# Gated delta attention between two spline layers: the values' tanh, the last passes of the next unit and the turned keys take other places in a written order

## What is computed

```python
qkvz = (x @ W_qkvz)                     # q, k, v (2 heads), z (2 heads) per key head
q, k, v = silu(causal_conv4(q, k, v))   # 4 taps along the tokens
q, k = INV**2 * rms_norm(q), INV * rms_norm(k)
def step(S, inp):                       # over the 512 tokens
    S = S * exp(g_t)
    delta = (v_t - k_t @ S) * beta_t
    S = S + outer(k_t, delta)
    o = q_t @ S
out = (silu(z) * rms_norm(o) * norm_w) @ W_out
x = x + out
```

## Time and profile before

| what | value |
|---|---|
| median of 3 runs | 3598.28 us (3597.3 to 3602.36) |
| the profiled execution's own time | 3600.39 us |
| its span | 3598.6 us |
| PE (matmul) busy | 3364.6 us, 93% |
| DVE busy | 2293.9 us, 64% |
| ACT busy | 2106.6 us, 59% |
| POOL busy | 2267.9 us, 63% |
| granted TensorE clock, mean | 0.978 |

### The profile page before, as it was taken

One profiled execution on the slowest core, in us unless ns is written; L12 is line 12 of the kernel. 1 busy time (PEld: TensorE's weight loads), 2 busy tenths in 40 slices (PEclk: granted clock), 3 DMA queues, 4 the chain that ended last, 5 costly groups with the idle time before them and its releaser, 6 DMA issues. The chain is left out here.

```text
span 3598.6 us, 77659 instructions
## 1 busy us (share of the span) xinstructions
PE 3364.6 (93%) x29092; PEld 2467.3 (69%) x29092; DVE 2293.9 (64%) x4402; ACT 2106.6 (59%) x5699; POOL 2267.9 (63%) x2680
## 2 busy tenths in 40 slices
PE   5997799999999999999999999999999999995998
PEld 3886366767676777667676767676767676773787
DVE  4664666666666767666666666666666666663564
ACT  3443566666666666666666666666666666662343
POOL 2111677777777777777777777777777777772110
PEclk8998899999999999999999999999999999997999
DMA  3524121212121212222222222222222222112321
GB/s 135 184 48 70 46 69 57 97 56 92 58 89 60 89 60 88 68 86 67 80 67 79 71 76 75 72 79 68 79 68 79 69 80 67 60 60 81 137 48 36
DMA packets 217314, 274.48 MB, mean 76 GB/s; under 512 B 91248, under 2 KB 127344, under 8 KB 215792
## 3 DMA queue, kind: packets, MB, share of 16 engines
q1 hardware_dynamic: 207680, 253.60, 22.6%
q0 software_dynamic: 4464, 14.36, 1.1%
q10 hardware_dynamic: 4800, 1.56, 0.3%
HBM read 180.12 MB, written 89.16 MB: 75 GB/s over the span
## 5 line engine op out<-in xcount | busy, mean ns | idle before, releaser
L2097 ACT ACTIVATE at_t<-at_inv 128x512 f16<-128x512 f32 x768 | 462.5, 602 | 398.1 <-PE at_inv L1905 391.9
L2337 DVE TENSOR_TENSOR at_pml<-at_prod,at_cst 128x256 f16<-128x256 f32 x768 | 323.0, 421 | 146.2 <-PE at_prod L1682 137.3
L2483 POOL TENSOR_TENSOR at_gm<-at_cst,at_gates 128x512 fp32r<-128x512 f32 x256 | 261.5, 1042 | 233.5 <-PE at_misc L1682 233.5
L1682 PE MATMUL at_proj<-x_hi,at_w_hi 128*128 128x512 f16 x1024 | 390.6, 381 | 2.8 <-PEq L1268 2.8
L1682 PE MATMUL at_proj<-x_lo,at_w_hi 128*128 128x512 f16 x1024 | 391.5, 382 | 0.0
L1682 PE MATMUL at_proj<-x_hi,at_w_lo 128*128 128x512 f16 x1024 | 391.5, 382 | 0.0
L2259 DVE SCALAR_TENSOR_TENSOR rows<-at_misc,first_tab,rows 128x512 f32<-128x512 f32 x256 | 191.7, 749 | 245.9 <-PE at_misc L1682 245.9
L1903 PE MATMUL at_inv<-at_pml,at_t 128*128 128x64 f16 x3072 | 286.8, 194 | 31.9 <-DVE at_pml L2337 31.6
L1903 PEld LDWEIGHTS at_inv<-at_pml,at_t 128*128 128x128 f16 x3072 | 223.1, 98 | 136.0 <-DVE at_pml L2337 83.3
L2215 DVE SCALAR_TENSOR_TENSOR at_cv_v<-at_proj,at_cw,at_cv_v 128x511 f32<-128x511 f32 (+2 forms) x384 | 287.5, 749 | 21.8 <-ACT at_cv_v L2021 8.3
L1682 PE MATMUL at_prod<-at_t,at_nlhi 128*128 128x64 f16 (+1 forms) x3584 | 287.8, 197 | 6.4 <-ACT at_t L2097 3.2
(11 more groups left out here) (323 smaller groups left out, 10278.4 us busy)
## 6 DMA issues: line engine op xcount, KB each, us to landing
rows<-x SPq DMA_DIRECT2D x64, 1024.0 KB, 5.5
x<-rows SPq DMA_DIRECT2D x64, 1024.0 KB, 4.6
at_gb<-decays SPq DMA_DIRECT2D x64, 512.0 KB, 3.7
at_raw_w<-w_qkvz SPq DMA_DIRECT2D x48, 512.0 KB, 7.5
ffn_weights<-ffn_w SPq DMA_DIRECT2D x1, 11776.0 KB, 34.8
ffn_w<-ffn_weights POOLq DMA_DIRECT2D x4, 2688.0 KB, 23.5
at_raw_o<-w_out SPq DMA_DIRECT2D x16, 512.0 KB, 3.5
f_xnext<-x_in SPq DMA_DIRECT2D x4, 1024.0 KB, 5.2
```

Source lines behind the costliest of these rows:

```text
L1682: return nc.tensor.matmul(out, lhsT, rhs, start=start, stop=stop)
L2097: own["a_t"].up(A(grown(t16[:, s % R].rearrange("p a t -> p (a t)"), s // R), grown(psT[s % R], s // R), ACT.Copy))
L2337: own["d_p"].up(V.tensor_tensor(pml[:, level - 1, g].rearrange("p (c b a m) -> p c b a m", c=CH, a=2, m=m)[:, :, :, 0, :], psP[:, 0:S // 2 ...
L2483: last = G.tensor_tensor(gm[:, k], incl.unsqueeze(1).to_broadcast([P, CH, P]), new_gates[:, g, at:at + CH, h:h + 1].to_broadcast([P, CH, P ...
```

## The change

On PE, the six `fill` lists of steps 11 to 15 are dealt out anew: Z1's 24 passes end as before in step 13 but lie 4, 4, 2 in place of 5, 2, 3 in steps 11 to 13; `turn_k` goes from step 12 to step 11; V0's 12 passes go from 4 and 8 in steps 14 and 15 to 2, 3, 3, 4 in steps 12 to 15. On ACT, V1's tanh leaves step 5 and stands at the end of the slot before, between the last squares of `at_aqk` and `copy_t(j + 1, 1)`; K's tanh goes from step 6 to step 4, ahead of `gated(j - 1, 1)`; Z0's from step 9 to step 8; `square_k` from step 12 to 11. On DVE, `silu_z(Z0)` goes from step 12 to step 10. POOL's and SP's passes are not edited.

```diff
@@ -1848,18 +1848,20 @@
                     fill[8].append(gates_in(Z1_U, 0, 5))
                     fill[9].append(gates_in(Z1_U, 5, 10))
                     fill[10].append(gates_in(Z1_U, 10, 14))
-                    fill[11].append(gates_in(Z1_U, 14, 19))
-                    fill[12].append(gates_in(Z1_U, 19, 21))
-                    fill[13].append(gates_in(Z1_U, 21, 24))
+                    fill[11].append(gates_in(Z1_U, 14, 18))
+                    fill[12].append(gates_in(Z1_U, 18, 22))
+                    fill[13].append(gates_in(Z1_U, 22, 24))
                 if behind:
                     for h in range(R):
                         fill[3 + 2 * h].append(lambda h=h: turn_gated(h, j - 1))
                     for c in range(WPROD):
                         fill[7 + c].append(lambda c=c: out_product(c, j - 1))
                 if has_prep:
-                    fill[12].append(turn_k)
-                    fill[14].append(parts(V0_U, 0, 4))
-                    fill[15].append(parts(V0_U, 4, 12))
+                    fill[11].append(turn_k)
+                    fill[12].append(parts(V0_U, 0, 2))
+                    fill[13].append(parts(V0_U, 2, 5))
+                    fill[14].append(parts(V0_U, 5, 8))
+                    fill[15].append(parts(V0_U, 8, 12))
                     gap[0].append(parts(V1_U, 0, 3))
                     gap[1].append(lambda: gram_of(j + 1))
                     gap[2].append(lambda: decay(0))
@@ -2118,18 +2120,17 @@
                 if has_prep:
                     steps[2].append(lambda: tap(Q_U))
                 if behind:
-                    for h in range(R):
-                        steps[2 + 2 * h].append(lambda h=h: gated(j - 1, h))
-                if has_delta:
-                    steps[5].append(lambda: tanh(V1_U, j - 1))
+                    steps[2].append(lambda: gated(j - 1, 0))
                 if has_prep:
-                    steps[6].append(lambda: tanh(K_U))
+                    steps[4].append(lambda: tanh(K_U))
+                if behind:
+                    steps[4].append(lambda: gated(j - 1, 1))
                 if has_prep:
                     steps[9].append(lambda: tanh(Q_U))
                 if has_delta:
-                    steps[9].append(lambda: tanh_z(Z0_U))
+                    steps[8].append(lambda: tanh_z(Z0_U))
                 if has_prep:
-                    steps[12].append(square_k)
+                    steps[11].append(square_k)
                 if has_delta:
                     steps[14].append(lambda: tanh_z(Z1_U))
                 for s in range(R, STEPS + 1):
@@ -2186,6 +2187,8 @@
                     for h in reversed(range(R)):
                         own["a_sqo"].up(squares(CH - 1, h))
                 if has_prep:
+                    tanh(V1_U)
+                if has_prep:
                     copy_t(j + 1, 1)
                 if ends:
                     for h in range(R):
@@ -2325,7 +2328,7 @@
                     for c in range(WPROD):
                         steps[7 + c].append(lambda c=c: out_add(c, j - 1))
                 if has_delta:
-                    steps[12].append(lambda: silu_z(Z0_U))
+                    steps[10].append(lambda: silu_z(Z0_U))
                 for s in range(R, STEPS):
                     if has_delta:
                         g, level = s % R, s // R
```

## The result

The changed kernel takes **3582.69 us** (median of 4 runs, 3576.59 to 3586.05) against 3598.78 of the kernel before (median of 4 runs, 3597.3 to 3602.36): a ratio of 0.995, 95% interval 0.9936 to 0.9964. That is 16.1 us less; 3587 was forecast, 11 less than the 3598.28 that the three runs had on which the forecast was made. The profiled execution took 3586.05 in place of 3600.39, its span is 3584.2 in place of 3598.6: 14.3 and 14.4 less.

A forecast was written before the change was run, and what follows sets the result against it. Slots were taken as paced by PE's instruction stream plus small waits, split slots by POOL's list. 63 slots losing 0.57 (+36 us) and split slots giving 46.5 make -11 us: 3598.28 to 3587, range 3562 to 3604.

The forecast's parts named there:

- The sum: Whole kernel: 63 middle slots lose 0.57 each, +36 us, split slots give back 46.5 us, together -11 us.
- 46.5 us of the split slots gone: 15 split slots, 3.1 us each over an ordinary slot's 43.87, become like the others: -46.5 us.
- The price of an ordinary slot: In each middle slot `turn_kn` comes at 1529.49 against 1528.92, 0.57 us later; +36 us over 63 slots.
- POOL leaves the path: POOL gains 3.3 us of lead, so it no longer delays `scale_k` in ordinary or split slots.
- the rival in which POOL does not come out early: Split slots keep their wait while each slot pays 0.57, +36 us: 3634; chance 0.05.
- The clock: PE: waits of 0.8 bring no fall, seven split-slot falls go; rival: falls in ordinary slots, 3634, chance 0.06.
- were taken out of the one place where a chain of ACT had to be covered: Between residual(1) and `turn_kn`, V0's eight passes become four; PE has 0.87 us less work and waits about 0.8.
- the four transposes fit into the wait for the mask: PE's step 11: `turn_k`'s four transposes, swapped for one pass, fit into the wait for DVE's mask.
- the lower bound of the price: Slot price 0.25 us if ACT's 0.29 wait for POOL and a similar slack at residual(1) come off: 3567.
- My first rival: Passes fill the waits of steps 12 and 13, ordinary slots stay at 43.9, only 46.5 us go: 3552; chance 0.12.

The follow-up runs named there:

- experiment 1: Kernel before with only V1's tanh moved to the slot's end and K's to step 4, no pass or silu moved: 3524.08 us, ratio 0.9795.
- experiment 2: The full change with V1's tanh back in step 5, K's back in step 6 and the gates as before: 3630.72 us, ratio 1.0091.
- experiment 7: experiment 1 plus `turn_k` in step 11 and Z1's passes 4, 4, 2; squares, silu and V0 stay: 3537.0 us, ratio 0.9841.
- (4): experiment 3 with Z0's silu also back in step 12 on DVE: 3555.43 us, ratio 0.9883.
- experiment 3: The full change with V0's passes back to 4 and 8 in steps 14 and 15: 3579.74 us, ratio 0.995.
- experiment 5: Kernel before with V1's tanh alone moved to the slot's end, K's tanh left in step 6: 3536.27 us, ratio 0.9837.

## Why the prediction was right, and where it was not

**The sum, against what was found.** In the beat: 46.5 us of the split slots gone, forecast and found (56 of its 61 slots, split or not, take 44.34 to 44.41, and five ordinary ones 44.49 to 44.68). The price of an ordinary slot was forecast as 0.57, and is 44.385 less 43.865, **0.52**. Over 61 slots that makes 46.5 less 31.7, 14.8, against 14.0 between the first and last rows of the beat (the longer slots are some of the rest); the forecast had 46.5 less 36 for 63 slots, 10.6. So the beat gives some 3 us more than forecast. Outside the beat the sum had no more than the price of two slots, and there are three terms: the first slot is 3.9 shorter, the phase starts 1.6 later (433.78 against 432.19), and 1.9 is lost behind the beat's last start (16.3 earlier, 3197.4 to 3181.1, where the span is shorter by 14.4). 14.0 + 3.9 - 1.6 - 1.9 is the 14.4 of the spans. That the three nearly cancel each other is luck. The medians are 16.1 apart, 1.7 more than the profiled executions: two runs of the changed kernel took 3576.59 and 3579.54, two 3585.84 and 3586.05, the last of which is the profiled one. What the two shorter ones did otherwise, no trace shows.

**The first slot was missing in the sum.** I counted every slot as an ordinary or a split one, and it is neither: its wait of POOL for V1's tanh was 7.95, twice the usual, and it had a fall of the clock of its own, the eighth beside the seven of the split slots. Against its 3.9 stands what is lost at the end of the phase, where the changed kernel has a stretch at the lower clock (columns as above):

```profile
3228.00:3232.00 4.00, 3.76 (x40) 3.21 (x38) 1.67 (x4) 2.49 (x5) 3.84 (x5) 0.57 0.00 0
```

The kernel before has none in its last slots up to 3260 (its granted clock is 1.00 from 3224 to 3260), and behind that both have two such stretches of equal length, 6.8 and 47.8. One fall more, at the 1.5 of the split slots, would be most of the 1.9; no run shows that it is.

**POOL leaves the path, right.** Experiments 1 and 2 show it from both sides: with the tanhs moved the split slots are as short as the others, with or without the passes; with the passes moved alone they stay longer. For the rival in which POOL does not come out early, 3634, experiment 2 is the nearest kernel, with 3630.7.

**The clock, right here.** There were seven falls in split slots and none is left; waits of 0.8 bring none in 62 slots. The Trainium skill ("TensorE: Matmul & The Clock Gate", "HAM oscillation — how this bites in real kernels") tells of a loop whose clock is throttled anew in every turn, but there each turn's wait is longer than its work. A slot here is 44 us long and its longest wait was 2.8 before and is 0.8 now for `turn_kn`, so no run here shows that case.

**The price of 0.57, right in size and wrong in what makes it.** The rows come where the forecast put them, within 0.04. Wrong is what I said of single pieces. I wrote that V0's passes "were taken out of the one place where a chain of ACT had to be covered", as if that made the price, and that the four transposes fit into the wait for the mask, which they do only while the silu makes that wait longer. The slots of the experiments take it apart, from the 43.46 with the tanhs alone to the 44.385 of the full change, 0.92:

| step | slot | adds |
|---|---|---|
| tanhs alone (1) | 43.46 | |
| + `turn_k` in step 11, Z1 4, 4, 2 (7) | 43.68 | 0.22 |
| + squares in step 11, Z0's tanh in 8 (4) | 43.97 | 0.29 |
| + Z0's silu in step 10 of DVE (3) | 44.35 | 0.38 |
| + V0's passes in steps 12 to 15 (the change) | 44.385 | 0.03 |

The slots are medians of the ordinary ones. V0's passes are nearly free where the others stand as they do. The costs hide each other: the updates of step 11 come 0.60 later in experiment 3 than in experiment 1, the silu's whole length, but 0.22 of that is there already in experiment 7, from `turn_k`'s wait for `out_add`, and 0.38 is left for the silu. residual(0)'s wait is covered by V0's passes. In another order of the steps the same pieces would get other prices.

**The term that the sum could not see.** Against the kernel before, the price was set against an ordinary slot of 43.87, which had 0.41 to give once the tanhs are moved: with them alone it falls to 43.46. I counted the 0.29 that ACT waited for POOL only in the lower bound of the price. In the change this gain is bought and given back within the same slot, as `turn_kn` hangs on `inverse_out(0)` in place of POOL. My first rival, "the waits vanish without a new one", 3552, was the nearest to what the move could bring, and still 28 us above experiment 1.

## What to carry to other kernels

When one edit frees a path and three others fill waits, cost each of the three alone against the kernel in which the first has been made: what a wait is worth is read from that kernel, not from the one before. Filling a wait with an instruction pays only if what moves is not itself late; here `turn_k`, `square_k` and `silu_z` each waited for something, or made the copy or mask behind them wait. And look at the first turn of a loop by itself: here the same wait was twice as long there as in the others, and brought a fall of the clock.

## What the runs showed of the hardware that I had not expected

The fall of the clock is not decided by the one long wait alone. Split slots with a wait of 2.8 ahead of `turn_kn` had a fall in 7 of 15 cases, those of experiment 2 with a wait of 2.4, a shorter one, in 13 of 15, at the same price of 1.5 us. (Waits as PE's weight loads show them; on PE itself they are 2.6 and 2.2.) The first slots of both kernels, where residual(1) waits 2.6 and 2.4 on PE, have one each. No middle slot with a wait of 0.8 had one, nor the split slots of experiment 5, with 0.5 to 0.7. What differs in experiment 2 ahead of the wait is where V0's passes and the small waits lie; which of these decides was not tried.
